# Feed-forward matmuls as pairs of 64-row halves, and another order of the work within two steps

## The reference, cut to what matters

```python
def reference(...):
    xn = _layernorm(x, axis=-1)
    return x + attn(xn) + ffn(xn)

def attn(x):                      # b = 4, n = 2048, H = 16 heads, Dh = 16
    q, k, v = split(x @ Wq + bq), split(x @ Wk + bk), split(x @ Wv + bv)
    q, k = _rope(q), _rope(k)
    scores = einsum('bhnd,bhmd->bhnm', q, k) / sqrt(d)
    weights = softmax(scores)
    inter = einsum('bhnm,bhmd->bhnd', weights, v)
    return inter @ Wo + bo

def ffn(x):                       # k0: 512x1024, k1: 1024x1024, k2: 1024x256, as +1 or -1
    h = concatenate([x, -x])
    h = relu(s0 * (h @ k0)) * 2
    h = relu(s1 * (h @ k1)) * 2
    return s2 * (h @ k2)
```

## Time and profile before

| What | Value |
|---|---|
| median of 3 runs | 2984.65 us (2983.89 to 2989.23) |
| the profiled execution's own time | 2983.02 us |
| span of its trace | 2981.2 us |
| TensorE busy | 2785.1 us, 93% |
| ScalarE busy | 2146.0 us, 72% |
| VectorE busy | 1057.8 us, 35% |
| mean granted TensorE clock | 0.973 |

### The profile page before, as it was taken

The page is one execution under the profiler, slowest core; times in us unless marked ns, Lnnn a source line. Parts: engine busy times, 40 slices in busy tenths (PEclk is TensorE's granted clock), DMA queues, the critical chain, the costliest instruction groups (busy, mean ns, idle before and its releaser), DMA issues.

```text
span 2981.2 us, 48065 instructions
## 1 busy us (share of the span) xinstructions
PE 2785.1 (93%) x16839; PEld 1300.0 (44%) x16839; DVE 1057.8 (35%) x1609; ACT 2146.0 (72%) x2301; POOL 376.9 (13%) x309
## 2 busy tenths in 40 slices
PE   6777299999999999999999999999999999999997
PEld 3443144444444444444444444444444444444444
DVE  7999422323232323232232323232322223232322
ACT  4446277777777777777777777777777777777773
POOL 5888300000000000000000000000000000000000
PEclk9999699999999999999999999999999999999998
DMA  6666411112121212112122212121211212221212
GB/s 200 196 196 191 131 43 44 43 47 55 47 50 41 61 45 73 49 46 62 48 65 54 69 44 69 39 75 45 63 53 51 62 47 66 54 69 43 74 35 96
DMA packets 279684, 211.62 MB, mean 71 GB/s; under 512 B 183616, under 2 KB 227392, under 8 KB 272960
## 3 DMA queue, kind: packets, MB, share of 16 engines
q1 hardware_dynamic: 271040, 200.30, 24.6%
q10 hardware_dynamic: 8448, 8.39, 0.9%
HBM read 132.08 MB, written 76.55 MB: 70 GB/s over the span
## 4 chain that ended last, share of the span: by engine, by line
PE 79%; issue 6%; DMA 2%; SPq 1%; DVE 1%; POOL 0%; ACT 0%; POOLq 0%; DVEq 0%
PE ps_o L871 29%; PE ps_f L903 27%; PE ps_s L856 22%; SPq L749 1%; DMA y<-rest_sum_d 1%; POOL heads L962 0%; PE ps_f L943 0%; DMA q_rows<-row_shift 0%; DVE sums L983 0%; DMA rest_sum_d<-rest_sum 0%; DMA probs<-rest_sum_d 0%; DMA heads_t<-heads 0%; DVE k_rows L1029 0%; PE ps_o L943 0%; DVE h_hi L993 0%
## 5 line engine op out<-in xcount | busy, mean ns | idle before, releaser
L831 ACT ACTIVATE probs<-ps_s 128x1024 f32<-128x1024 f32 x2048 | 1985.8, 1022 | 620.5 <-PE ps_s L856 620.5
L871 PE MATMUL ps_o<-probs,v_ones 128*32 128x512 f32 x8192 | 992.0, 602 | 0.0
L856 PE MATMUL ps_s<-q_rows,k_rows 50*128 50x512 f32 x4096 | 797.0, 462 | 61.9 <-DMA q_rows<-row_shift 32.6
L856 PEld LDWEIGHTS ps_s<-q_rows,k_rows 50*128 50x128 f32 x4096 | 337.2, 185 | 717.3 <-ACT probs L831 468.1
L993 DVE TENSOR_SCALAR h_hi<-ps_f 128x512 fp32r<-128x512 f32 x256 | 175.7, 686 | 1102.1 <-PE ps_f L903 1101.7
L903 PE MATMUL ps_f<-h_hi,ffn_w 128*128 128x512 f32 x1024 | 425.8, 416 | 0.0
L903 PE MATMUL ps_f<-h_lo,ffn_w 128*128 128x512 f32 x1024 | 415.6, 406 | 0.0
L871 PEld LDWEIGHTS ps_o<-probs,v_ones 128*32 128x32 f32 x8192 | 214.6, 109 | 453.0 <-issue 449.6
L962 POOL TENSOR_TENSOR heads<-heads,sums 128x512 f32<-128x512 f32 x64 | 85.9, 1342 | 2240.1 <-DVE sums L983 2240.1
L903 PEld LDWEIGHTS ps_f<-h_hi,ffn_w 128*128 128x128 f32 x1024 | 192.1, 188 | 101.7 <-issue 70.1
L983 DVE RECIPROCAL sums<-sums 128x128 f32<-128x128 f32 x256 | 225.0, 920 | 1.8
(11 more groups left out here) (87 smaller groups left out, 1382.5 us busy)
## 6 DMA issues: line engine op xcount, KB each, us to landing
k_rows<-k_parts SPq DMA_DIRECT2D x128, 256.0 KB
q_rows<-q_parts SPq DMA_DIRECT2D x384, 64.0 KB
q_parts<-parts SPq DMA_DIRECT2D x32, 512.0 KB, 3.7
k_parts<-parts SPq DMA_DIRECT2D x32, 512.0 KB, 4.5
k_rows<-k_parts SPq DMA_DIRECT2D x128, 128.0 KB
x_chunk<-in_x ACTq DMA_DIRECT2D x16, 512.0 KB, 4.1
xn_t<-xnT SPq DMA_DIRECT2D x16, 512.0 KB, 4.4
v_heads<-v_sb SPq DMA_DIRECT2D x16, 512.0 KB, 5.3
```

What stands on the lines that cost most here:

```text
L831: nc.scalar.activation(probs[:, s % PBUF, half * 2 * C:(half + 1) * 2 * C], ps_s[:, half].rearrange("p c n -> p (c n)"), ACT.Exp, scale=SC ...
L856: last = nc.tensor.matmul(ps_s[:, half, w], k_rows[rows, u, t * P:(t + 1) * P], q_rows[rows, u, half], start=True, stop=True)
L871: last = nc.tensor.matmul(ps_o[32 * c:32 * c + 2 * DH], v_ones[:, u, t], probs[:, s % PBUF, c * C:(c + 1) * C], start=(t == 0), stop=(t == ...
```

## The change

It has three parts.

1. **Halves.** Each feed-forward matmul of 128 rows is replaced by two matmuls of 64 rows. Two groups (`pair`, sides 0 and 1) run together: in phase 0 array rows 0 to 63 work for side 0 and rows 64 to 127 for side 1, each on a bank of its own; in phase 1 they change sides, so that each side gets both halves of its rows. Between the phases the queue waits on a new semaphore `half_done`. The number of 512-column time slots is what it was, with two matmuls in each. The projection keeps its 128 rows.
2. **Order.** `turns` is replaced by `cycles`. With S a half of scores and F a run of feed-forward matmuls, a cycle was S S F S S and two weighings; it is now S S F S F S and two weighings.
3. **Deal.** A table `VISITS` says how many slots each of the two F of a cycle holds. The first layer takes 4 cycles (slots 4 and 4 in each), the projection 2 (4 matmuls and 0; empty in passes without projection), the second layer 4 times five cycles (4 2, 4 3, 3 3, 4 2, 4 3), the third 2 times three (7 4, 5 5, 7 4, of 256 columns). VectorE takes both sides of a pair when both are done.

```diff
+VISITS = {FIRST: [4, 4], PROJECT: [4, 0], SECOND: [4, 2, 4, 3, 3, 3, 4, 2, 4, 3], THIRD: [7, 4, 5, 5, 7, 4]}
...
-            def scores(i, s):
+            def scores(i, s, half):
...
-                if m == 0:
-
-                    pe.wait_ge(group_used, before + (k_th + 2 if k_th < BANKS - 1 else k_th + 1))
+                if m == 0:
+
+                    pe.wait_ge(group_used, before + (first + 3 if first == 0 else first + 2))
...
+                size = 2 * (DT if layer == FIRST else FT)
+                phase, part = m // size, m % size
+                k, low = part // 2, part % 2
+                swap = SWAPS * i + pair + {FIRST: 0, SECOND: FT // 2, THIRD: FT}[layer] + 1
+                if m == size:
+                    pe.wait_ge(half_done, 2 * swap)
+                for w in range(2):
+                    side = (w + phase) % 2
+                    rows = slice(GROUP_ROWS * w, GROUP_ROWS * (w + 1))
+                    n = 2 * pair + side
+                    if layer == FIRST:
+                        to, lhs, rhs = ps_f[:, banks[side]], w0[rows, k, n * P:(n + 1) * P], (xT_hi, xT_lo)[low][rows, k]
...
+                    last = nc.tensor.matmul(to, lhs, rhs, start=(m == 0), stop=(m == 2 * size - 1))
...
-                for s in range(FFN_FROM, STEPS + FFN_FROM, 2):
-                    if s < STEPS or not last:
-                        scores(i, s)
-                    for n, m in TURNS[projects][s] + TURNS[projects][s + 1]:
-                        beside(i, projects, n, m)
-                    if s < STEPS or not last:
-                        scores(i, s + 1)
+                for c in range(STEPS // 2):
+                    s = FFN_FROM + 2 * c
+                    more = s < STEPS or not last
+                    if more:
+                        scores(i, s, 0)
+                        scores(i, s, 1)
+                    for layer, pair, m in TURNS[projects][2 * c]:
+                        beside(i, projects, layer, pair, m)
+                    if more:
+                        scores(i, s + 1, 0)
+                    for layer, pair, m in TURNS[projects][2 * c + 1]:
+                        beside(i, projects, layer, pair, m)
+                    if more:
+                        scores(i, s + 1, 1)
                     weigh(i, s - 2)
                     weigh(i, s - 1)
```

More of the change, by code:

```diff
@@ L61, with pairs, number, cycles @@
 GROUPS = SUMS + TT
[L64 to L87, removed]
+SWAPS = FT + TT // 2
+FIRST, PROJECT, SECOND, THIRD = range(4)
+def pairs(layer):
+    return {FIRST: FT // 2, PROJECT: TT // 2, SECOND: FT // 2, THIRD: TT // 2}[layer]
+def number(layer, pair, side):
+    return {FIRST: 0, PROJECT: GROUPS, SECOND: FT, THIRD: SUMS}[layer] + 2 * pair + side
+VISITS = {FIRST: [4, 4], PROJECT: [4, 0], SECOND: [4, 2, 4, 3, 3, 3, 4, 2, 4, 3], THIRD: [7, 4, 5, 5, 7, 4]}
+def cycles(with_projection):
+    visits, ends, order = [], [], []
+    for layer in (FIRST, PROJECT, SECOND, THIRD):
+        for pair in range(pairs(layer)):
+            at = 0
+            for count in VISITS[layer]:
+                present = layer != PROJECT or with_projection
+                visits.append([(layer, pair, at + m) for m in range(count)] if present else [])
+                at += count
+            ends += [[] for _ in VISITS[layer][::2]]
+            if layer != PROJECT or with_projection:
+                ends[-1] = [number(layer, pair, side) for side in range(2)]
+                order += ends[-1]
+    assert len(ends) == STEPS // 2
+    return visits, ends, {n: k for k, n in enumerate(order)}
+TURNS, ENDS, ORDER = zip(*(cycles(p) for p in (False, True)))
 def groups_before(i, projects):
@@ L845, in _ @@
         def _(pe):
-            def scores(i, s):
+            def scores(i, s, half):
                 j, t = s // KT, s % KT
                 u = j % 2
-                if t == 0:
+                if t == 0 and half == 0:
                     pe.wait_ge(rows_loaded[u], 16 * LOADS * 2 * i + 16 * LOADS * (j // 2 + 1))
[L852 to L858, removed]
+                pe.wait_ge(probs_ready, 2 * STEPS * i + (2 * s + half + 1))
+                for w in range(2):
+                    rows = slice(GROUP_ROWS * w, GROUP_ROWS * w + ROWS)
+                    last = nc.tensor.matmul(ps_s[:, half, w], k_rows[rows, u, t * P:(t + 1) * P],
+                                            q_rows[rows, u, half], start=True, stop=True)
+                last.then_inc(scores_ready, 1)
             def weigh(i, s):
@@ L891, in beside @@
[L891 to L902, removed]
@@ L903, in beside @@
-                last = nc.tensor.matmul(to, lhs, rhs, start=(m == 0), stop=(m == size - 1))
-                if m == size - 1:
-                    last.then_inc(group_done, 1)
-            def one_pass(i, projects, last=False):
-                for s in range(FFN_FROM, STEPS + FFN_FROM, 2):
-                    if s < STEPS or not last:
-                        scores(i, s)
-                    for n, m in TURNS[projects][s] + TURNS[projects][s + 1]:
-                        beside(i, projects, n, m)
-                    if s < STEPS or not last:
-                        scores(i, s + 1)
+                if pair == 0 and layer in (SECOND, THIRD) and m in (0, 2 * (FT - 2)):
+                    sums_of = (FIRST, SECOND)[layer == THIRD]
+                    needed = FT // 2 - 1 if m else FT // 2 - 2
+                    pe.wait_ge(group_used, before + (ORDER[projects][number(sums_of, needed, 1)] + 1 + BANKS))
@@ new lines, in beside @@
+                if layer == PROJECT:
+                    side, k = m // DT, m % DT
+                    t = 2 * pair + side
+                    last = nc.tensor.matmul(ps_f[:, banks[side], 0:D], headsT[:, k, t * P:(t + 1) * P], wo[:, k],
+                                            start=(k == 0), stop=(k == DT - 1))
+                    if k == DT - 1:
+                        last.then_inc(group_done, 1)
+                    return
+                size = 2 * (DT if layer == FIRST else FT)
@@ L917, in one_pass @@
                     weigh(i, s - 2)
                     weigh(i, s - 1)
+            w0, w1, w2 = w["w0"], w["w1"], w["w2"]
             pe.sem_inc(pv_done, PBUF)
-            scores(0, 0)
-            scores(0, 1)
+            for s in range(FFN_FROM):
+                scores(0, s, 0)
+                scores(0, s, 1)
             pe.wait_ge(consts_loaded, 48)
```

31 lines of the change are left out of this document (19 added, 12 removed).

## The result

| | Time | Ratio to the kernel before, 95% interval |
|---|---|---|
| the kernel before | 2984.57 us, median of 4 | |
| the changed kernel | 3006.64 us, median of 4 (3003.30 to 3009.63) | 1.0069 (1.0053 to 1.0085) |

The change made the kernel 22 us slower, 0.7%. The forecast was 2996, slower, with 2975 to 3015 as its range. The profiled execution took 3009.63, 26.6 more than the profiled one of before. It is the slowest of the four and the one of before lies 1.6 under its median, so 26.6 is the difference of the two traces, and 22 that of the kernels.

The account below looks back on a forecast made before the run. The prediction took a loop through ScalarE to close cycles of six at 4.90, with TensorE bounding those of seven. Terms +16.5 +3.8 +5.0 +4 +1.2 -17.4 -0.6 gave +12.5 on 2983.0, 2995.5; forecast 2996, range 2975 to 3015.

Parts of the forecast that it names:

- rival (4): Pair dearer than 0.23 (at 0.27, +33: 3029) or seams go badly (new dips, +10: 3006); chance 0.15.
- signs of being wrong: New profile: loop cycles under 4.85, pair pace off 0.23, TensorE waiting for `half_done` or `group_used`, seams moved over 10 us.
- The unit prices: TensorE: 0.23 per pair of halves, 0.20 per change of array division, 0.40 of drains removed per cycle.
- rival (2): ScalarE loop gets shorter: first exponential after 0.54 everywhere, some 450 cycles lose 0.08, -36 to 2960; chance 0.05.
- First layer +16.5: First-layer cycles with 4 and 4 slots take 5.15, 0.26 over the loop, 64 times.
- three slots +3.8: Cycles with three slots in the second run take 4.92 against 4.90: 192 x 0.02.
- projection +5.0: Projection cycles take 5.10: two cycles of +0.20 in each of 12 passes.
- The wait for y, +4: First projection matmul comes 0.7 earlier while `y` lands unmoved; four waiting passes wait longer, two or so begin to.
- Two banks, +1.2: Passes 4 and 15, starting without a jump: a pair waits for VectorE to empty a side, +1.2 for two.
- half_done, nothing: Wait between phases costs nothing behind the third half of scores; uncovered, about 0.3 per pair, 48 us.
- Saved, -18: Cycles of seven and the fifth cycle drop to the loop in 12 projection passes, -17.4; pass 15, -0.6.
- the term for the seams: Pass starts: no general shift in the sum; better seams some -12, chance 0.22, new dips +10 within a 0.15 chance.

Follow-up runs that it names:

- the two short-exponential kernels: The kernel before and the changed kernel, each with exponentials over 512 columns in place of 1024 (the other half of `probs` holds 1): 2949.5 and 2814.3 us.
- `fitted`: The changed kernel with slots redealt in all layers to what the ScalarE loop leaves room for, projection 3 0 1 0: 2964.1 us, 0.9948 of the kernel before.
- `one_run`: The changed kernel with both feed-forward runs of a cycle joined, S S F S S: 3003.3 us, 1.0071 of the kernel before.
- `no_empty`: The changed kernel with the empty cycles of passes 0 to 3 filled by first-layer slots 2 2 2 2 for two pairs: 2990.1 us, 1.0031 of the kernel before.
- `short_exp_after`: The changed kernel with each exponential over 512 columns in place of 1024, the other half of `probs` holding 1: 2814.3 us, one run.

## Why the prediction was right, and by how much it was short

The time is 10.6 over the forecast. It lies inside the range of 2975 to 3015, but 2.6 above the forecast's own range of 2986 to 3004, where rival (4) had put new dips at the seams, 3006. That rival's other half, the dearer pair, did not come true. So the direction and the cost of the cycles were read rightly, and the seams were not. Two of the signs of being wrong did show: the pass starts moved by 11.9 together, more than the 10 named, and TensorE waited for `group_used`, though only the two times that the sum itself had. There is also a slip in the last step: 2995.5 and 1.6 make 2997, not 2996.

**The bound.** Right, and shown by the two short-exponential kernels: a cycle stands on first scores, two exponentials, fourth half, two weighings, 4.90 in all, whatever lies between, as long as it fits.

**The unit prices.** Right: 0.23 for a pair (1233.48, 1233.71), no drain between scores and feed-forward work (0.57), third half at 1.70 (I had its load at 1.69), cycles of 4.90 to 4.92, 5.15 and, for the projection, 5.11 (5.10 forecast). TensorE's idling before the third half is 0.27 (0.30 forecast). Rival (4)'s dearer pair falls, and so does rival (2), as the first exponential still comes 0.62 after the scores.

**First layer +16.5, three slots +3.8, projection +5.0.** As forecast by these cycle times, and shown a second time by `fitted`, which takes them back and lands 1 us from its forecast.

**The wait for y, +4.** Measured +3.3 in the waits; with slower clock behind the longest ones it is somewhat more.

**Two banks, +1.2.** VectorE waited for 1.2, twice; the two cycles behind those starts are 5.83 instead of 5.15, 1.4 together.

**half_done, nothing.** Right; 0.36 where its cover is gone, measured in `one_run`, against 0.3 (48 us) in the text.

**Saved, -18.** Right; no cycle of seven is left at 4.98.

**What the sum lacked** is in the term for the seams, which I left at zero and gave to rival (4) with +10 and a chance of 0.15. The profiled execution is 26.6 over the one before, the sum had 12.5, so 14.1 are missing.

- The fifth to seventh cycles of passes 0 to 3 took 7.5. The two sparse cycles were priced as if a wait were only its own length: in five of eight their idling of some 0.96 and 0.41 was followed by the lower clock for the weighings, 1.65 more per cycle in pass 1. That is shown three times: by the trace, by `no_empty`, where the cycles are filled and the loss is gone, and by `short_exp_after`, where the same empty cycles idle less and keep the high clock.
- The pass starts took 130.8 against 118.9, 11.9 more. The sum had 2.8 of it: 3.9 for 15 longer first-layer cycles, less 1.1 for the twelve cycles of seven that stood there. So 9.1 were not in it. Of the 11.9, longer idling makes 5.7 (28.4 and 3.3 became 32.5 and 4.9); the rest is the longer cycle and the lower clock. That the starts became longer is seen in one trace of each kernel; why they did stays open.

Together this is 16.6, or 2.5 more than is missing: the other terms came out 2.5 below the sum. For the first three pass starts the reason is not the projection, as there is none in those passes.

## What to carry to other kernels

A busy share of 93% and a chain of 79% do not prove that an engine sets the time. Look for two places where the same instructions run with a different interval (4.82 and 4.90 here), and for one block that takes 0.67 in one place of a cycle and 0.80 in another: there another engine may close the loop. When a change frees an engine inside such a loop, the gain is room, not time, and it becomes time only when more work is put into each turn: the same halves in the same order are 0.7% slower with one table of slots and 0.5% faster with another (`fitted`). And once the cycles are all at the loop's length, look at the seams: two passes in each turn of TensorE's loop gave 18 us in the kernel before and 34 in the fitted one.

## What the runs showed of the hardware that was not expected

- A pair of 64-row fp32r halves that accumulate in two banks runs at 0.23, the pace of one 128-row matmul, and of one scores pair; in 256 columns 0.12. Nothing before had shown an accumulating pair.
- A pass start with a jump back of TensorE's loop is 2 to 8 longer here than one without: up to 3.6 of idle time, then in some cases a second stall of up to 2.4 within the first cycle, and weighings at the lower clock. Only the idle time shows in the waits, as "issue".
- Of eight cycles with an idle stretch of 0.77 to 0.97 and another of 0.41 or 0.42 among their matmuls, five lost the high clock. The cycles with one stretch of 0.27 (the second-layer cycle shown) or 0.54 (the empty ones of `short_exp_after`) did not.
